# One transformer layer on one core: results of experts 0 to 6 gathered during the last expert, the last expert's results placed by products with a 0/1 matrix

## The reference, cut to what matters

```python
x = x + xattn(layernorm(x), ctx_1024, ...)   # self attention, cross attention over 16 x 1601 keys, a ReLU pair
x = x + rglru(layernorm(x), ...)             # gates, causal convolution, a recurrence over time, output product
x = x + ffn(layernorm(x), ...)               # mixture of experts, below; T = 1024 tokens of D = 512

def ffn(x, gate_w, gate_proj_w, up_proj_w, down_proj_w):      # E = 8 experts, K = 2 of them for a token, H = 1024
    probs = softmax(xf @ gate_w.T); top_p, top_i = top_k(probs, 2)
    w = top_p / (sum(top_p) + 1e-9)
    rank = cumsum(one_hot(top_i), axis=0) - 1                 # apart for the first and the second choice
    keep = my_rank < int(1.25 * T / E)                        # 160 tokens for each expert and choice
    for e in range(E):
        y = (silu(xf @ gate_proj_w[e].T) * (xf @ up_proj_w[e].T)) @ down_proj_w[e].T
        out = out + comb[:, e:e+1] * y                        # comb = w * keep at (token, expert)
```

## Time and profile before

| | us |
|---|---|
| median of three timed runs | 1120.21 |
| the profiled execution, whole | 1121.53 |
| its span (first to last instruction) | 1119.5 |
| PE busy | 1033.4 |
| DVE busy | 562.7 |
| ACT busy | 382.2 |
| POOL busy | 185.6 |

### The profile page before, as it was taken

The page is one execution under the profiler, slowest core; times in us unless marked ns, Lnnn a source line. Parts: engine busy times, 40 slices in busy tenths (PEclk is TensorE's granted clock), DMA queues, the critical chain, the costliest instruction groups (busy, mean ns, idle before and its releaser), DMA issues.

```text
span 1119.5 us, 13822 instructions
## 1 busy us (share of the span) xinstructions
PE 1033.4 (92%) x5191; PEld 763.7 (68%) x5191; DVE 562.7 (50%) x1093; ACT 382.2 (34%) x604; POOL 185.6 (17%) x174
## 2 busy tenths in 40 slices
PE   6999899999999999777999999999999999999970
PEld 3454444444444487665888888799999999999960
DVE  4046332323333387593636666455555555665624
ACT  1211121211111323134557740344444444444410
POOL 2001400000000156242522121600000000000005
PEclk9999999999999999997999998999999999999995
DMA  9833299989999622012321100674554554544307
GB/s 326 341 118 148 95 360 407 388 354 407 406 404 410 211 62 59 1 48 66 112 68 43 34 10 7 238 261 150 187 191 140 188 173 156 187 161 143 109 23 225
DMA packets 38659, 207.55 MB, mean 185 GB/s; under 512 B 5248, under 2 KB 6784, under 8 KB 34384
## 3 DMA queue, kind: packets, MB, share of 16 engines
q1 hardware_dynamic: 33216, 187.98, 45.9%
q0 software_dynamic: 5392, 18.88, 4.8%
HBM read 190.07 MB, written 16.78 MB: 185 GB/s over the span
## 4 chain that ended last, share of the span: by engine, by line
PE 81%; DVE 10%; POOL 3%; DMA 3%; issue 1%; ACT 1%; POOLq 0%; SPq 0%; DVEq 0%; ACTq 0%
PE ps L825 20%; PE ps L609 19%; PE ps L841 11%; PE ps L426 8%; PE ps L536 8%; PE ps L562 7%; DMA big<-in_ctx 2%; PE ps L759 1%; POOL big L1739 1%; DVE big L1258 1%; PE ps L520 1%; DVE stats L1128 1%; DVE big L1391 1%; PE ps L564 1%; PE ps L433 1%
## 5 line engine op out<-in xcount | busy, mean ns | idle before, releaser
L825 PE MATMUL ps<-x,w 128*128 128x320 f32 x1536 | 237.2, 311 | 1.1 <-DVE x L1613 1.1
L825 PEld LDWEIGHTS ps<-x,w 128*128 128x128 f32 x1536 | 228.5, 188 | 5.3 <-issue 1.6
L1571 DVE TENSOR_TENSOR w<-big,w 128x1536 fp32r<-128x1536 f32 x64 | 112.4, 1758 | 94.5 <-ACT w L1064 93.9
L1668 POOL TENSOR_TENSOR u<-big,u 128x512 fp32r<-128x512 f32 (+1 forms) x44 | 63.9, 1460 | 389.9 <-ACT u L923 389.9
L841 PE MATMUL ps<-w,hsplit 128*128 128x512 f32 x512 | 128.1, 393 | 0.0
L426 PE MATMUL ps<-big 128*128 128x512 f32 x240 | 106.8, 605 | 11.2 <-DMA big<-in_wk1T 10.4
L1064 ACT CAST w<-big 128x1536 fp32r<-128x1536 f32 x64 | 94.4, 1478 | 43.9 <-PE ps L841 42.9
L536 PE MATMUL ps<-big 128*64 128x512 f32 (+2 forms) x512 | 102.9, 505 | 2.7 <-DMA big<-in_ctxT 1.2
L841 PEld LDWEIGHTS ps<-w,hsplit 128*128 128x128 f32 x512 | 93.5, 188 | 16.7 <-DVE hsplit L1600 0.2
L609 PE MATMUL ps<-xcT,u 128*128 128x512 f32 x432 | 98.1, 389 | 0.0
L609 PEld LDWEIGHTS ps<-xcT,u 128*128 128x128 f32 x432 | 81.1, 188 | 16.8
(11 more groups left out here) (215 smaller groups left out, 1266.2 us busy)
## 6 DMA issues: line engine op xcount, KB each, us to landing
big<-in_ctxT SPq DMA_DIRECT2D x16, 3202.0 KB, 14.5
big<-in_ctx SPq DMA_DIRECT2D x16, 3072.0 KB
big<-in_w_units SPq DMA_DIRECT2D x64, 768.0 KB, 4.3
big<-in_dense_units SPq DMA_DIRECT2D x42, 256.0 KB, 2.7
xs<-big POOLq DMA_DIRECT2D x1, 5120.0 KB, 24.8
big<-in_gate_units SPq DMA_DIRECT2D x12, 384.0 KB, 3.0
ys<-big POOLq DMA_DIRECT2D x8, 512.0 KB, 3.3
hr<-xs SPq DMA_DIRECT2D x7, 512.0 KB, 5.2
```

What stands on the lines that cost most here:

```text
L825: mm = nc.tensor.matmul(ps[:, 2 * part + f % 2, 0:SLOTS], wsplit[f % RING][w][:, c:c + P], xsplit[j][x][:, d, :], start=(d == 0 and w + x ...
L1571: V.tensor_tensor(wsplit[f % RING][1][:], wraw[f % RING], wsplit[f % RING][0][:].bitcast(F32), ALU.subtract).then_inc(w_low, 1)
L1668: G.tensor_tensor(low[:, 0:w], uraw[u % 4][:, 0:w], high[:, 0:w].bitcast(F32), ALU.subtract).then_inc(u_low, 1)
```

## The change

1. **Experts 0 to 6.** Their results are gathered and added while the last expert runs. POOL stores expert 6 (`store(NE - 2, 0)`), waits for the stores, and issues the same 16 gathers. DVE adds tile i by `mix(i)`, two multiply-adds as before, at the end of a step of the last expert: tile 0 in step 3, tile 1 in step 4, tiles 2 and 3 in step 5, tiles 4, 5, 6 in step 6, tile 7 in step 7. The buffers' wait is now on `mixed`, counted by `mix`.
2. **Expert 7** is not stored. `route_weights` takes its tokens' weights out of `rt[:, 1]` into `mx` and sets their gather row to 0. In steps 2 to 6 of expert 0, DVE makes `pick_last` (tokens by slots of expert 7, 5 comparisons; its tiles lie in `lnw`). In the last expert, PE turns it tile by tile through bank 7 (3 transposes in each step, between `gate_up` and `down`), and ACT copies each turned tile to `pick_lastT` (8 copies).
3. **After the last `down`** ACT and DVE split the three result tiles into high and low, PE forms for each token tile the sum of 3 x 2 products (0/1 matrix by high and by low, 48 in all), and DVE adds `mx` times that, read from PSUM, to `xr`.

```diff
 PE
+            def transpose_picks(i):
+                pe.wait_ge(picked, 3 + NT // 2)
+                if i:
+                    pe.wait_ge(pick_out, i)
+                for s in range(NS):
+                    mm = nc.tensor.transpose(ps[:, 7, s * P:(s + 1) * P], pick_last[:, i, s * P:(s + 1) * P], ident[:])
+                mm.then_inc(pick_done, 1)
+            def last_rows(i, s):
+                b = (0, 1, 2, 3, 7, 0, 1, 2)[i]
+                if s == 0:
+                    pe.wait_ge(pick_out, i + 1 if i < 4 else NT)
+                    if i > 4:
+                        pe.wait_ge(out_ready, i - 4)
+                pe.wait_ge(last_low, s + 1)
+                for part in range(2):
+                    mm = nc.tensor.matmul(ps[:, b, :], pick_lastT[:, s, tok(i)], y_last[part][:, s, :],
+                                          start=(s == 0 and part == 0), stop=(s == NS - 1 and part == 1))
+                if s == NS - 1:
+                    mm.then_inc(last_filled, 1)
...
+                    if last:
+                        transpose_picks(f)
-                    down(n, f, first)
+                    down(n, f, first, last and f == FC - 1)
...
+            for s in range(NS):
+                for i in range(4):
+                    last_rows(i, s)
+            for i in range(4, NT):
+                for s in range(NS):
+                    last_rows(i, s)
 ACT
+            def picks_out(i):
+                act.wait_ge(pick_done, i + 1)
+                nc.scalar.copy(pick_lastT[:, :, i * P:(i + 1) * P],
+                               ps[:, 7, 0:NS * P].rearrange("p (s t) -> p s t", t=P)).then_inc(pick_out, 1)
...
+                    if last and f:
+                        picks_out(f - 1)
...
-            tail_out(NE - 1)
+            picks_out(NT - 1)
+            act.wait_ge(y_out[1], 32 * (NE // 2 - 1))
+            for s in range(NS):
+                act.wait_ge(last_done, s + 1)
+                nc.scalar.copy(y_last[0][:, s, :], ps[:, 4 + s, :]).then_inc(last_high, 1)
 DVE
+                to_last = oh[:, :, NE - 1]
+                rt_chained(V.tensor_tensor(rt[:, 6, :], rt[:, 1, :], to_last, ALU.mult))
...
+                V.tensor_tensor(gath[:], rt[:, 7, :], rt[:, 2, :], ALU.subtract).then_inc(idx_done, 1)
+            def pick_last_rows(i):
...
+                V.tensor_tensor(pick_last[:, i:i + 2, 0:SLOTS].rearrange("p i (k s) -> p i k s", s=CAP), ids,
+                                r3[5][:, i:i + 2, :].unsqueeze(3).to_broadcast([P, 2, TOPK, CAP]),
+                                ALU.is_equal).then_inc(picked, 1)
...
+                    if first and 2 <= f < 2 + NT // 2:
+                        pick_last_rows(2 * (f - 2))
+                    if first and f == FC - 2:
+                        pick_last_again()
                     if f in (2, 4, 5) and not last:
                         slots_low(n + 1, 1 - j, (f - 1) // 2 if f < 5 else 2)
+                    if last:
+                        for i in range(*((0, 0), (0, 0), (0, 0), (0, 1), (1, 2), (2, 4), (4, 7), (7, 8))[f]):
+                            mix(i)
...
-            results_out(NE - 1, 1, NE // 2 - 1)
+            for s in range(NS):
+                dve.wait_ge(last_high, s + 1)
+                V.tensor_tensor(y_last[1][:, s, :], ps[:, 4 + s, :], y_last[0][:, s, :].bitcast(F32),
+                                ALU.subtract).then_inc(last_low, 1)
+            for i in range(NT):
+                dve.wait_ge(last_filled, i + 1)
+                dve.wait_ge(mixed, i + 1)
+                V.scalar_tensor_tensor(xr[:, i, :], ps[:, (0, 1, 2, 3, 7, 0, 1, 2)[i], :], mx[:, i:i + 1], xr[:, i, :],
+                                       ALU.mult, ALU.add).then_inc(out_ready, 1)
 POOL
-            with pool.Fori(0, NE // 2) as i:
+            with pool.Fori(0, NE // 2 - 1) as i:
...
+            store(NE - 2, 0)
...
-                    pool.wait_ge(out_ready, i - 3)
+                    pool.wait_ge(mixed, i - 3)
```

More of the change, by code:

```diff
@@ L246, in perceiver_program @@
         yg = [at(33920 + j * 2 * D, TOPK, D) for j in range(4)]
-        ytail = at(38016, D)
+        ytail = at(3072, D)
+        pick_last = lnw[:, 0:6, :].rearrange("p r d -> p (r d)").rearrange("p (i s) -> p i s", s=NS * P)
+        pick_lastT = rounded("pick_lastT", 10240, NS, T)
+        y_last = [rounded("y_last_high", NS * D, NS, D), rounded("y_last_low", 28800, NS, D)]
         ye = [at(j * NS * D, NS, D) for j in range(2)]
@@ L251, in perceiver_program @@
         xs = nc.dram_tensor("xs", (TRASH + TOPK * T, D), F32, kind="Internal").ap()
-        ys = nc.dram_tensor("ys", (TRASH, D), F32, kind="Internal").ap()
+        ys = nc.dram_tensor("ys", (TRASH - SLOTS, D), F32, kind="Internal").ap()
         x_in = [sem(f"x_in{j}") for j in range(4)]
@@ L289, in perceiver_program @@
         yg_in = [sem(f"yg_in{j}") for j in range(4)]
-        mix_step, out_ready, out_done = map(sem, ("mix_step", "out_ready", "out_done"))
+        mix_step, mixed, out_ready, out_done = map(sem, ("mix_step", "mixed", "out_ready", "out_done"))
+        pick_done, pick_out, last_done, last_high, last_low, last_filled = map(
+            sem, ("pick_done", "pick_out", "last_done", "last_high", "last_low", "last_filled"))
         def unit_home(u):
@@ L828, in gate_up, with down @@
                     mm.then_inc(gu_done, 1)
-            def down(n, f, first=False):
+            def down(n, f, first=False, final=False):
                 pe.wait_ge(hid_low, n["n"] * (2 * FC) + (2 * f + 2))
@@ L842, in down @@
                                               stop=(f == FC - 1 and k == len(terms) - 1))
-                mm.then_inc(down_done, 1)
+                    if final:
+                        mm.then_inc(last_done, 1)
+                if not final:
+                    mm.then_inc(down_done, 1)
+            def transpose_picks(i):
[17 more added lines that the diff above has]
+                    mm.then_inc(last_filled, 1)
             def expert(n, j, nxt, first=False, last=False):
@@ L1565, in route_weights, with pick_last_again, mix @@
                 rt_chained(V.scalar_tensor_tensor(rt[:, 7, :], rt[:, 3, :], float(CAP), rt[:, 4, :], ALU.is_le, ALU.mult))
-                V.tensor_copy(gath[:], rt[:, 7, :]).then_inc(idx_done, 1)
+                to_last = oh[:, :, NE - 1]
+                rt_chained(V.tensor_tensor(rt[:, 6, :], rt[:, 1, :], to_last, ALU.mult))
+                V.tensor_tensor(rt[:, 2, :], rt[:, 7, :], to_last, ALU.mult).then_inc(rt_step, 1)
+                V.tensor_tensor(mx[:], r3[6][:, :, 0], r3[6][:, :, 1], ALU.add).then_inc(rt_step, 1)
+                V.tensor_scalar(rt[:, 5, :], rt[:, 4, :], float((NE - 1) * SLOTS), None, ALU.subtract).then_inc(rt_step, 1)
+                rsteps[0] += 3
+                rt_chained(V.tensor_tensor(rt[:, 1, :], rt[:, 1, :], rt[:, 6, :], ALU.subtract))
+                V.tensor_tensor(gath[:], rt[:, 7, :], rt[:, 2, :], ALU.subtract).then_inc(idx_done, 1)
+            def pick_last_rows(i):
+                ids = slot_ids.rearrange("p (k s) -> p k s", s=CAP).unsqueeze(1).to_broadcast([P, 2, TOPK, CAP])
+                V.tensor_tensor(pick_last[:, i:i + 2, 0:SLOTS].rearrange("p i (k s) -> p i k s", s=CAP), ids,
+                                r3[5][:, i:i + 2, :].unsqueeze(3).to_broadcast([P, 2, TOPK, CAP]),
+                                ALU.is_equal).then_inc(picked, 1)
+            def pick_last_again():
+                V.tensor_tensor(pick_last[:, :, SLOTS:SLOTS + LAST],
+                                slot_ids[:, SLOTS - LAST:SLOTS].unsqueeze(1).to_broadcast([P, NT, LAST]),
+                                r3[5][:, :, 1].unsqueeze(2).to_broadcast([P, NT, LAST]), ALU.is_equal).then_inc(picked, 1)
+            def mix(i):
+                dve.wait_ge(yg_in[i % 4], 32 * (i // 4 + 1))
+                for k in range(TOPK):
+                    V.scalar_tensor_tensor(xr[:, i, :], yg[i % 4][:, k, :], rt[:, 1, TOPK * i + k:TOPK * i + k + 1],
+                                           xr[:, i, :], ALU.mult, ALU.add).then_inc(mixed if k else mix_step, 1)
+                    if k == 0:
+                        dve.wait_ge(mix_step, i + 1)
             def split_low(n, f, first=False):
@@ L1727, in store @@
                 pool.dma_start(rows[(NS - 1) * P:SLOTS, :], ye[j][0:LAST, NS - 1, :]).then_inc(y_out[j], 16)
-            with pool.Fori(0, NE // 2) as i:
+            with pool.Fori(0, NE // 2 - 1) as i:
                 for j in range(2):
                     store(i * 2 + j, j)
-            for j in range(2):
-                pool.wait_ge(y_out[j], 32 * (NE // 2))
+            store(NE - 2, 0)
+            pool.wait_ge(y_out[0], 32 * (NE // 2))
+            pool.wait_ge(y_out[1], 32 * (NE // 2 - 1))
             pool.wait_ge(idx_done, 3)
```

6 lines of the change are left out of this document (removed).

## The result

The changed kernel takes 1102.11 us (median of four runs, 1100.0 to 1102.76), the kernel before 1120.49 in four runs beside it. The ratio is 0.984, with a 95% interval of 0.9815 to 0.9862: 18.4 us less, where 16.7 were forecast. The profiled execution took 1102.76 us, its span 1100.9, 18.6 less than before.

A forecast was written before the change was run, and what follows sets the result against it. TensorE was taken to bound the last expert, with a tail behind it: 36.2 us go, 1.1 + 2.3 + 1.2 + 14.9 come, so 16.7 less than 1120.2 gives 1103.5 us. Own range 1100 to 1107; 8 in 10, 1099 to 1110.

The forecast's parts named there:

- What bounds it, and what goes: TensorE bounds the last expert; the 36.2 us tail of move-out, store, gathers, multiply-adds and output behind it goes.
- Term 1: Expert 0: added VectorE work makes TensorE stand before the third turn in step 4, 1.1 us (bounds 0 to 1.4).
- a sign of being wrong: Expert 0, step 4: TensorE's stand before the third turn being 0 instead of about 1.1 us.
- Term 2: Last expert: three transposes per step cost 0.33 us, 2.3 us over steps 0 to 6; step 7's hide.
- up to 1107: Transposes at their full duration, or another small loss, take the time up to 1107 us; chance 0.03.
- Term 3: Last expert: gathers and multiply-adds make VectorE late, so TensorE waits 1.2 us ahead of the last `down` (bounds 0 to 3.0).
- Term 4: New tail: splitting, 48 placing products, additions and store, 14.9 us from the last `down`'s end to 1101.7.
- Gathers late: Last expert: slower gathers make VectorE wait 1.5 and then 0.6 us, 2.1 us in all, to 1105.6; chance 0.18.
- Clock in the tail: TensorE's clock falls for the placing products: 1112.7 us for all, 1105.3 if back after 4 us; chance 0.10.
- Slower by the landing: Last expert: slow gather landings delay step 7's tile, eating the whole gain at 16.7 us each; chance 0.03 with like waits.
- The cheap entry: VectorE's waits absorb the added work in expert 0 and the last expert: 2.3 us less, 1101.2 us; chance 0.08.

The follow-up runs named there:

- e6: Changed kernel with the gathers made to wait for the last expert's end and the multiply-adds one by one ahead of the final additions: 1120.00 us.
- e10: The changed kernel run once more, unchanged: 1103.09 us; the table with it sets ScalarE's wait for the load against the length of expert 0's stretch.
- e1: Changed kernel without its 24 transposes in the last expert, ScalarE's copies kept: 1101.06 us.
- e2: Changed kernel with tile 3's multiply-adds moved from step 5 to step 6 of the last expert, so four tiles stand there: 1104.87 us.
- e7: Changed kernel with gathers still early but all multiply-adds behind the last expert, ahead of the final additions: 1113.09 us.
- e5: Changed kernel with three idle comparisons added on VectorE in steps 2, 3 and 4 of expert 0: 1106.90 us.
- e11: Changed kernel with three idle comparisons in steps 2, 3 and 4 of expert 0, run a second time: 1109.24 us (one run).
- e9: Changed kernel with two idle comparisons added on VectorE in step 4 of expert 0: 1105.39 us.

## Why the prediction was right, point by point

- **What bounds it, and what goes.** Right. The 36.2 us behind TensorE's end are gone, and e6 shows that it is the place of the gathers and their multiply-adds that counts: 16.7 of the 18.7 us.
- **Term 1, 1.1 us: right mechanism, mis-sized by about 1 us, and 0 in this execution.** In the changed kernel's first profile the low part for the third turn was there 0.5 us ahead (759.10 + 0.68 against 760.28), which the prediction itself named as a sign of being wrong. That it was exactly 0 is the luck of a load in time; the runs show 0 to 1.0. But the load does not explain the 1.1. It was worked out from the earlier trace rows, an execution in which ScalarE waited 0.95 us for the load, and at such a load the table under e10 gives 0.1 to 0.2 us. Two sizes were wrong. The five new small operations cost 0.68 us in place of 1.0, since those that don't depend on each other start 0.08 us apart and not 0.2. And VectorE's idle time took up some 1.0 us of the added work in place of 0.3: ahead of step 4's weight split it had waited 1.84 us for ScalarE, and with the change 0.82. First the row of before, then those of the changed kernel:

```profile
756.05 1.76 DVE L1571 TENSOR_TENSOR w<-big,w 128x1536 fp32r<-128x1536 f32 x1 [1.84 <-ACT w L1064]
```

```profile
756.69 1.76 DVE L1648 TENSOR_TENSOR w<-big,w 128x1536 fp32r<-128x1536 f32 x1 [0.82 <-ACT w L1103]
...
759.10 0.68 DVE L1654 TENSOR_TENSOR x<-ps,x 128x512 fp32r<-128x512 f32 x1
...
760.28 0.43 PE L814 MATMUL ps<-ident,hr 64*128 64x64 f32 x2
```

- **Term 2, 2.3 us: right.** The chain has 0.33 us for three transposes in each step. In all eight it is 2.6: step 7's do not hide, as the wait that was to hide them did not come. In this trace a transpose's row is 0.272 us long, and what it costs is 0.11, as in the earlier trace rows. No run shows the term behind the forecast's "up to 1107", transposes that cost their full duration: rows of 0.272 us, three to a step, lengthened a step by 0.33. e1 qualifies the term: taken away, the transposes give back 1.4 us, since VectorE is next.
- **Term 3, 1.2 us: the step that was mis-sized; it measured 0.** VectorE's lateness was followed in the right order, but hidden tile 6 came at 1076.06 in place of 1076.8, and tile 7 at 1081.89, on time, in place of 1083.0. Of these 1.1 us, half lies in the multiply-adds: each token tile was taken at 1.54 us, and from start to start six of them cost 1.45 each (1077.54 to 1081.89 for three). Another 0.2 is the hidden tile's low part, there 1.48 us behind the tile's start in steps 5 and 6 and not 1.6; the rest is step 4's weight split, which could start at 1068.55, 0.35 sooner than the working needs. And there was slack where the term had none: in e2 tile 7 is 1.41 us later, and TensorE only 1.08.
- **Term 4: right.** From the last `down`'s start to the end 1100.9 - 1083.9 = 17.0 us, 1101.7 - 1084.8 = 16.9 predicted. The products took 0.232 us each (11.15 in all), 0.2375 predicted; they started 2.5 us behind the last `down`'s start in place of 2.2, and the two differences cancel.
- **The sum.** 16.7 predicted, 18.6 in the span: 1.1 more from term 1 and 0.9 more from terms 2 and 3 together (2.6 against 3.5), less the 0.1 by which the experts began later.
- **The rivals.** Gathers late: 0.32 us once, covered. They landed sooner than in the earlier trace rows (median 3.6 against 4.5 us). GpSimd's gathers did slow beside VectorE, six of the 16, up to 1.55 us and once 2.142 against a median of 0.947, but they had the room; the section on the hardware shows which ones. Clock in the tail: 1.00 throughout. Slower by the landing: nothing. The cheap entry (1101.2) is what came, and it had 0.08; it deserved more, since both of its terms rested on slack of about a microsecond, read from one execution.

## What to carry to other kernels

Here the chain behind the last product (move-out, store, gathers, additions, output store) cost its whole length, 36.2 us. Under the last expert, which TensorE bounds, the gathers and multiply-adds cost TensorE at most 0.2 us (the last hidden tile 39.73 us behind the first, 39.55 in e6 and e7), since VectorE had room there. With four buffers the additions had to move along: the early gathers alone gave back 7.0 us, both together 16.7 (e6, e7). Only the last stage's part then needed another way out, and products with a 0/1 matrix on a TensorE that had been idle there did it in 11.15 us without a trip through HBM. Where two engines' chains met within tenths of a microsecond, the costs on them didn't add (e1: 1.4 us in place of 2.7). And slack read from one execution, 0.5 us ahead of the third turn, was worth no more than the jitter of the loads, for which ScalarE waited 0 to 1.77 us in the executions of the same code: compare several executions by stretches between fixed events. How much added work an engine's idle time takes up stands in the trace, wait by wait: here one wait of 1.84 us gave 1.0, where 0.3 was reckoned in all.

## What the runs showed of the hardware

**What makes a gather long.** Five rows of the changed kernel's last expert:

```profile
1056.74 0.95 POOL L1824 DMA_INDIRECT big<-ys,gath  x1 [0.30 <-issue]
1056.96 1.76 DVE L1648 TENSOR_TENSOR w<-big,w 128x1536 fp32r<-128x1536 f32 x1 [2.17 <-ACT w L1103]
...
1057.99 1.55 POOL L1824 DMA_INDIRECT big<-ys,gath  x1 [0.30 <-issue]
...
1071.67 0.48 DVE L1673 TENSOR_TENSOR big<-big,ps 128x320 f32<-128x320 f32 x1
1072.03 0.94 POOL L1824 DMA_INDIRECT big<-ys,gath  x1 [3.69 <-DVE xr L1640]
```

The gather at 1057.99 starts while VectorE's weight split runs, an operation with both inputs in SBUF (the core's working memory), and ends at 1059.54, 0.82 us behind the split's end. The one at 1056.74 started ahead of the split and took 0.95 beside it. The one at 1072.03 starts inside an operation that reads one input from PSUM (where TensorE's products arrive), and took 0.94. So it is in all 14 profiled executions, of 16 gathers each. 80 gathers start 0.09 us or more inside a VectorE operation with both inputs in SBUF, and each ends 0.81 to 0.82 us behind that operation's end (0.87 to 0.88 for the first of the 16); they took 1.14 to 2.54 us. The other 144, three of them begun less than 0.03 us inside such an operation, took 0.94 to 1.00. The 2.142 us of the first gather are this: the split ends at 1053.02, the gather at 1053.89.

By these rows the 80 gathers waited for VectorE's operation. In the other direction no wait is seen: the split at 1056.96 starts inside a gather and takes 1.76 us, where all 64 splits of this execution took 1.75 to 1.76.

**Other figures.**

- A product of 512 columns with operands that are not split: before, 64 of them at a granted clock of 1.00 started 0.43 us apart (L426, from 29.96 to 57.43). Those with split operands took 0.2375, and 0.232 among the placing products.
- A stand of 2.27 us, with one of 0.52 ten us before it, was followed by a granted clock of 0.50 for TensorE in one execution (e5, 1.6 us lost on top). In another of the same program (e11) stands of 2.28 and 0.36 were not. A stand of 1.66 us (e9) left it at 1.00.
- Gathers landed in a median of 3.6 us inside the last expert and 4.5 behind it; behind it, the output stores ran beside them.
